# Inverse square roots of the layer norms and of one root mean square: ScalarE's root and VectorE's reciprocal replaced by a power on GpSimd

## The reference, cut to what matters

```python
def _layernorm(x, axis=-1, eps=1e-05):
    m = jnp.mean(x, axis=axis, keepdims=True)
    v = jnp.var(x, axis=axis, keepdims=True)
    return (x - m) / jnp.sqrt(v + eps)

# inside the first attention (16 heads of 8 features, two softmaxes a1 - lam * a2):
out = jnp.einsum('bhst,bhtd->bhsd', a, v)
rms = jnp.sqrt(jnp.mean(out * out, axis=-1, keepdims=True) + EPS)      # EPS = 1e-6
out_n = out / rms * norm_w[None, :, None, :] * (1.0 - LAMBDA_INIT)

x = L0_attn_x
x = _layernorm(x + first_attention(x))
x = _layernorm(x + fp4_feed_forward(x))
x = _layernorm(x + second_attention(x))
x = _layernorm(x + experts(x))       # eight experts, top 1, with a layer norm of its own inside
return x
```

## Time and profile before

| | us |
|---|---|
| runs | 1400.9, 1401.93, 1407.16 |
| median | 1401.93 |
| span of the profiled execution, first to last instruction | 1405.9 |

### The profile page before, as it was taken

One profiled execution on the slowest core, in us unless ns is written; L12 is line 12 of the kernel. 1 busy time (PEld: TensorE's weight loads), 2 busy tenths in 40 slices (PEclk: granted clock), 3 DMA queues, 4 the chain that ended last, 5 costly groups with the idle time before them and its releaser, 6 DMA issues.

```text
span 1405.9 us, 20714 instructions
## 1 busy us (share of the span) xinstructions
PE 1159.2 (82%) x7625; PEld 587.0 (42%) x7625; DVE 798.6 (57%) x1864; ACT 669.1 (48%) x1489; POOL 417.6 (30%) x463
## 2 busy tenths in 40 slices
PE   2588668799898698899988788899988598899686
PEld 1123222334454334444454434445455365455454
DVE  4697449665775665634776575643875521765312
ACT  1178316672663346663574255664375133266132
POOL 2000112204874022002775022000776300577000
PEclk7599656889998679999998769999999699999799
DMA  5700120000030000000030000000000000000000
GB/s 142 180 3 3 63 43 2 1 10 1 19 80 1 1 2 2 2 2 16 1 98 1 1 2 1 2 2 8 0 2 1 0 1 0 9 1 1 1 0 8
DMA packets 30933, 25.07 MB, mean 18 GB/s; under 512 B 12329, under 2 KB 27761, under 8 KB 30065
## 3 DMA queue, kind: packets, MB, share of 16 engines
q1 hardware_dynamic: 30832, 23.75, 6.6%
HBM read 16.01 MB, written 7.34 MB: 17 GB/s over the span
## 4 chain that ended last, share of the span: by engine, by line
PE 62%; DVE 17%; ACT 6%; POOL 5%; SPq 5%; issue 4%; DMA 1%; POOLq 0%; ACTq 0%; DVEq 0%
PE ps L1296 9%; PE ps L1199 9%; PE ps L1194 8%; PE ps L1323 6%; DVE mx L775 6%; PE ps L1279 6%; PE ps L1338 4%; PE ps L1358 4%; PE ps L1368 4%; PE ps L1430 2%; PE ps L1215 2%; SPq L396 2%; POOL PROB L459 2%; PE ps L1254 2%; PE ps L1309 1%
## 5 line engine op out<-in xcount | busy, mean ns | idle before, releaser
L775 DVE TENSOR_REDUCE mx<-ps 128x1 f32<-128x512 f32 x512 | 323.3, 683 | 149.5 <-PE ps L1254 147.6
L1033 ACT ACTIVATE PROB<-ps 128x512 f32<-128x512 f32 x512 | 276.3, 600 | 199.3 <-PE ps L1279 198.2
L459 POOL TENSOR_SCALAR PROB<-PROB,rsum 128x128 f32<-128x128 f32 (+3 forms) x224 | 229.2, 1036 | 58.8 <-DVE rsum L903 58.2
L1075 ACT ACTIVATE PROB<-ps,mx 128x128 f32<-128x128 f32 (+3 forms) x256 | 133.1, 526 | 152.6 <-DVE mx L898 152.4
L1254 PE MATMUL ps<-kst,qst 24*128 24x512 bf16 x512 | 157.5, 461 | 34.9 <-DVE mx L775 20.4
L1296 PE MATMUL ps<-PROB,v 128*32 128x256 f32 x2048 | 173.3, 427 | 2.7 <-ACT OREG L1042 2.3
L440 POOL CAST mparts<-mx 128x16 bf16<-128x16 f32 x32 | 6.3, 197 | 520.9 <-DVE mx L775 520.9
L1279 PE MATMUL ps<-qst,kst 27*128 27x512 bf16 x512 | 129.7, 434 | 28.7 <-DMA qst<-mrow 15.3
L898 DVE TENSOR_REDUCE mx<-ps 128x1 f32<-128x128 f32 (+3 forms) x256 | 112.9, 482 | 70.5 <-PE ps L1341 70.4
L1194 PE MATMUL ps<-xnT,w_sb 128*128 128x512 f32 x256 | 141.8, 659 | 7.2 <-DVE MREG L718 3.7
L995 ACT ACTIVATE MREG<-ps,b_sb 128x512 f32<-128x512 f32 x128 | 88.3, 690 | 121.7 <-PE ps L1194 121.3
(11 more groups left out here) (183 smaller groups left out, 1372.5 us busy)
## 6 DMA issues: line engine op xcount, KB each, us to landing
qk_terms<-RREG SPq DMA_DIRECT2D x48, 128.0 KB, 2.1
kst<-qk_terms SPq DMA_DIRECT2D x16, 192.0 KB
qst<-qk_terms SPq DMA_DIRECT2D x16, 192.0 KB
w_sb<-in_L_ffn_W_dram SPq DMA_DIRECT2D x1, 2048.0 KB
qst<-mrow SPq DMA_DIRECT2D x96, 4.0 KB
ZC<-in_L_attn_x_dram SPq DMA_DIRECT2D x4, 256.0 KB, 3.2
XN<-in_L_attn_x_dram SPq DMA_DIRECT2D x4, 256.0 KB, 9.4
out_dram<-XP SPq DMA_DIRECT2D x4, 256.0 KB, 2.3
```

The source lines that it names most:

```text
L459: pool.tensor_scalar(tile, tile, rsum1[:, 2 * v + half:2 * v + half + 1], None, ALU.mult).then_inc(scaled1, 1)
L775: dve.tensor_reduce(mx0[:, ga % 2, col:col + 1], ps[:, max_banks[MAX_SLOT[n] % len(max_banks)], :], AX, ALU.max, negate=True).then_inc(slo ...
L1033: act.activation(prob0[:, s % 2, q % 4, q % 8 // 4], ps[:, s0_banks[q % len(s0_banks)], :], ACT.Exp, scale=float(HD0) ** -0.5).then_inc(ex ...
L1075: act.activation(prob1[:, half, at:at + w], ps[:, a1_bank(v, half), 0:w], ACT.Exp, bias=mx1[:, col:col + 1], accum_out=sum1[:, col:col + 1 ...
```

## The change

ACT no longer takes any square root. For each of the places above POOL adds the epsilon (for the root mean square it also multiplies by 1/8) and raises the result to the power -0.5, as a power of two tensors, against a tile `root` that is filled with -0.5 at the start. DVE then multiplies by the result and takes no reciprocal. On POOL the new steps stand behind `scale_probs(r, 10)` and the bias add for the root mean square, behind `scale_probs(r, 19)` for the norm after the first attention, and in `overlap` behind `max_parts0(k, 5)` for the norm after the feed-forward, ahead of `max_parts0(k, 0)`, between it and `max_parts0(k, 1)`, and at the end for the three norms of the experts' half.

```diff
-        eps = sb("eps", [P, 2])
+        root = sb("root", [P, 4 * H0])[:, :]
...
@@ block.gpsimd
-            pool.memset(eps[:, 0:1], LN_EPS).then_inc(setup_pool, 1)
-            pool.memset(eps[:, 1:2], RMS_EPS).then_inc(setup_pool, 1)
+            pool.memset(root, -0.5).then_inc(setup_pool, 1)
...
+            def over_std(st, mv, n, var, std):
+
+                pool.wait_ge(var, n)
+                step(pool.tensor_scalar(st, mv[:, :, 1], LN_EPS, None, ALU.add)); settle()
+                pool.tensor_tensor(st, st, root[:, 0:NT], ALU.pow).then_inc(std, 1)
...
             def overlap(r):
-                k = r + 1
+                k, i = r + 1, r - 1
                 hidden = 0 <= r < BATCH
                 if hidden:
                     rounds = quantise(ha, hc, 1408, hq_ready)
+                if 0 <= i:
+                    over_std(stC, mvC, 3 * i + 1, varC, stdC)
                 for g in range(NG):
                     if k < BATCH:
                         max_parts0(k, g)
+                    if 0 <= i and g == 0:
+                        over_std(stC, mvC, 3 * i + 2, varC, stdC)
                     if hidden and g in (2, 3):
...
+                    if hidden and g == 5:
+                        over_std(stB, mvB, 2 * r + 2, varB, stdB)
+                if 0 <= i:
+                    over_std(stC, mvC, 3 * i + 3, varC, stdC)
 
             def turn(k, nx, v, rounds):
...
+                if k < BATCH and v == 10:
+                    pool.wait_ge(ms_ready, k + 1)
+                    step(pool.tensor_scalar(rms[:, 1], rms[:, 0], 1.0 / HD0, RMS_EPS, ALU.mult, ALU.add))
+                    settle()
+                    pool.tensor_tensor(rms[:, 1], rms[:, 1], root, ALU.pow).then_inc(rms_ready, 1)
+                if k < BATCH and v == 19:
+                    over_std(stB, mvB, 2 * k + 1, varB, stdB)
                 if nx < BATCH and v in (10, 13):
                     split_next(nx, (v - 10) // 3)
...
@@ block.vector
             def scale(src, dst, mv, st, std, n, done):
                 dve.wait_ge(std, n)
-                step(dve.reciprocal(st[:, 1], st[:, 0])); settle()
                 for t in range(NT):
-                    ins = dve.tensor_scalar(dst[:, t], src[:, t], mv[:, t, 0:1], st[:, 1, t:t + 1], ALU.subtract, ALU.mult)
+                    ins = dve.tensor_scalar(dst[:, t], src[:, t], mv[:, t, 0:1], st[:, t:t + 1], ALU.subtract, ALU.mult)
...
                 if v == 11:
                     dve.wait_ge(rms_ready, k + 1)
-                    step(dve.reciprocal(rms[:, 0], rms[:, 1]))
...
                 if v == 20:
                     dve.wait_ge(stdB, 2 * k + 1)
-                    step(dve.reciprocal(stB[:, 1], stB[:, 0])); settle()
...
@@ block.scalar
-            def std_b(n):
-                act.wait_ge(varB, n)
-                act.activation(stB[:, 0], mvB[:, :, 1], ACT.Sqrt, bias=eps[:, 0:1]).then_inc(stdB, 1)
-
-            def std_c(n):
-                act.wait_ge(varC, n)
-                act.activation(stC[:, 0], mvC[:, :, 1], ACT.Sqrt, bias=eps[:, 0:1]).then_inc(stdC, 1)
...
-                    if v == 10:
-                        act.wait_ge(ms_ready, k + 1)
-                        act.activation(rms[:, 1], rms[:, 0], ACT.Sqrt, bias=eps[:, 1:2], scale=1.0 / HD0).then_inc(rms_ready, 1)
-                    if v == 19:
-                        std_b(2 * k + 1)
```

More of the change, by code:

```diff
@@ L191, in build @@
         xq = XQ[:, :].rearrange("p (t n) -> p t n", t=NT)
-        bnB, mvB, stB = sb("bnB", [P, NT, 6]), sb("mvB", [P, NT, 2]), sb("stB", [P, 2, NT])
-        bnC, mvC, stC = sb("bnC", [P, NT, 6]), sb("mvC", [P, NT, 2]), sb("stC", [P, 2, NT])
+        bnB, mvB, stB = sb("bnB", [P, NT, 6]), sb("mvB", [P, NT, 2]), sb("stB", [P, NT])[:, :]
+        bnC, mvC, stC = sb("bnC", [P, NT, 6]), sb("mvC", [P, NT, 2]), sb("stC", [P, NT])[:, :]
         PROB = sb("PROB", [P, 2 * 4 * PW])
@@ L417, in _ @@
             pool.memset(kst[:, :, :], 1.0).then_inc(setup_pool, 1)
-            pool.memset(eps[:, 0:1], LN_EPS).then_inc(setup_pool, 1)
-            pool.memset(eps[:, 1:2], RMS_EPS).then_inc(setup_pool, 1)
+            pool.memset(root, -0.5).then_inc(setup_pool, 1)
+            pool.wait_ge(setup_pool, 5)
+            pool.memset(v0[:, :, :, HD0:HD0 + 1], 1.0).then_inc(setup_pool, 1)
             pool.wait_ge(setup_pool, 6)
-            pool.memset(v0[:, :, :, HD0:HD0 + 1], 1.0).then_inc(setup_pool, 1)
-            pool.wait_ge(setup_pool, 7)
             own = [0]
@@ L577, in scales @@
                     last.then_inc(done, 1)
-            dve.wait_ge(setup_pool, 7)
+            dve.wait_ge(setup_pool, 6)
             dve.wait_ge(first_in, 48)
@@ L822, in outputs0 @@
                     dve.wait_ge(rms_ready, k + 1)
-                    step(dve.reciprocal(rms[:, 0], rms[:, 1]))
                 if v == 12:
-                    settle()
-                    w = rms[:, 0].rearrange("p (g a) -> p g a", a=1).broadcast_to([P, 4 * 4 * NT, HD0])
+                    w = rms[:, 1].rearrange("p (g a) -> p g a", a=1).broadcast_to([P, 4 * 4 * NT, HD0])
                     step(dve.tensor_tensor(o0, o0, w, ALU.mult))
@@ L845, in input0 @@
                     dve.wait_ge(stdB, 2 * k + 1)
-                    step(dve.reciprocal(stB[:, 1], stB[:, 0])); settle()
                 if v in (20, 21):
                     for t in (2 * (v - 20), 2 * (v - 20) + 1):
-                        ins = dve.tensor_scalar(XA[:, t], ZB[:, t], mvB[:, t, 0:1], stB[:, 1, t:t + 1], ALU.subtract, ALU.mult)
+                        ins = dve.tensor_scalar(XA[:, t], ZB[:, t], mvB[:, t, 0:1], stB[:, t:t + 1], ALU.subtract, ALU.mult)
                         if t < NT - 1:
@@ L995, in experts_stream @@
                     act.activation(hE[:, f], ps[:, 5 + f % 2, :], ACT.Relu, bias=b1_sb[:, e, f:f + 1]).then_inc(relu_done, 1)
-                if (s, c) == (17, 3):
-                    std_c(3 * i + 3)
             def silu(r, t, bank):
@@ L1011, in ffn_stream @@
                     act.copy(hT[0:96, t % 2, 2, :], ps[0:96, 7, 256:384]).then_inc(hT_ready, 1)
-                if (s, c) == (9, 2):
-                    std_b(2 * r + 2)
                 if (s, c) == (10, 1):
@@ L1048, in turn @@
             def turn(k, nx, v):
-                if k < BATCH:
-                    if v == 10:
-                        act.wait_ge(ms_ready, k + 1)
-                        act.activation(rms[:, 1], rms[:, 0], ACT.Sqrt, bias=eps[:, 1:2], scale=1.0 / HD0).then_inc(rms_ready, 1)
-                    if v == 19:
-                        std_b(2 * k + 1)
                 if nx < BATCH:
```

## The result

The changed kernel takes 1462.82 us (median of four runs, 1460.9 to 1463.66) where the kernel before, run beside it, takes 1404.55 (four runs): a ratio of 1.0404, 95% interval 1.0372 to 1.0436. The profiled execution took 1460.9 us, with a span of 1459.1 us against 1405.9 before. The direction was forecast, the size was not: +15.5 us and a range to 1440.

What follows compares the result with a forecast made beforehand. TensorE carried 62% of the chain, so waits at the 24 root places counted, not ACT or POOL as bounds. Terms 9.9 + 4.5 + 2.4 + 1.75 - 0.8 - 2.2 gave +15.5 us on 1401.9, so 1417 us, range 1390 to 1440.

Steps and rivals of the forecast that it cites:

- x64: Time of POOL's power on 64 columns, for the root mean square: 1.5 us, between 0.32 and 2.8.
- The third rival: The power is done element by element, 10 us at 64 columns: 1456 us or far more; chance 0.12.
- A: Root mean square in the second attention's loop: +3.3 us in each of rounds 0 to 2, nothing in round -1.
- B: Norm after the first attention, v = 19, 20: +1.5 us in each of three rounds; round -1 only a longer hand-over.
- C1: First norm of the experts' half: PE's transpose waits for POOL, +1.2 us in each of rounds 1 and 2.
- hand-overs of B, C1 and C3: Where nothing else is late, DVE's scaling starts 0.85 us after the statistics instead of 0.58: +0.25 us at seven places.
- C3: Last norm of the experts' half: only a longer hand-over, +0.25 us in all four rounds.
- norm after the feed-forward, rounds 1, 2: Gives back most of PE's 1.23 us wait for ACT: 1.0 us gained in each of these rounds.
- the place term of 1.8: At A, DVE's maxima of v = 13 come 1.8 us later, plus x64, from the step's place in POOL's queue.
- The first rival: Loads come off and no wait shows; A gains 2.3 and B 2.4 us a round: 1389 us; chance 0.17.
- The estimate of 1370 us: By the skill page, two loads cost some 5.3 us per root; A and B alone would give 32 us.
- The second rival: PE's other queued work covers most of DVE's lateness; A costs 1, B 0 a round: 1406 us; chance 0.18.

Runs made afterwards that it cites:

- e1: Changed kernel with the 64-column power replaced by a product of the same shape (root mean square left out): 1418.9 us, ratio 1.009 to the kernel before.
- e7: Kernel before, with only the norms after the first attention (ahead of v = 18's products) and after the feed-forward as POOL powers: 1394.58 us, ratio 0.9916.
- e6: e1 with the short root-mean-square step moved ahead of scale_probs(10) and the bias add: 1418.34 us, ratio 1.009 to the kernel before.
- e8: e7 with the root mean square's sum of squares and ACT root moved ahead into the round's projections: 1402.9 us, ratio 0.9975 to the kernel before.
- e5: e1 with the twenty 4-column norm powers also replaced by products, so no root is computed: 1404.48 us, ratio 0.999 to the kernel before.
- e9: e7 with the power for the norm after the first attention moved behind v = 19's products: 1400.5 us, ratio 0.9977 to the kernel before.

## Why the prediction was right in direction and wrong in size

**The step that failed is the price of the power.** It was put "nearer the upper end than the middle of a plain add: x64 = 1.5 us", between bounds of 0.32 and 2.8, and at 0.35 for four columns. It measured 10.57 and 1.04. The upper bound took twelve passes at 3.45 ns a column of an ordinary two-operation form, 41 ns a column; the power takes 159. The row that the bound was scaled from shares nothing with a power but the engine, and a bound made so is none. The third rival, "The power is slow", had x64 at 10 us and 1456 us, with a chance of 0.12; it is what happened, and the sign named for being wrong, a power far from 1.5 us at 64 columns, came. Why a power takes that long no run shows.

With the two measured prices, the prediction's own terms give this, beside the shifts (us; each more than before):

| place | on record | same term, measured price | shift measured |
|---|---|---|---|
| A, rounds 0 to 2 | 3.3 each | 1.8 + 10.57 = 12.4 each | 13.7, 13.5, 14.4 |
| A, round -1 | 0 | 10.57 - 2 = 8.6 | 9.9 |
| B, rounds 0 to 2 | 1.5 each | 1.5 + 0.69 = 2.2 each | 0.3, 1.7, 1.9 |
| C1, rounds 1 and 2 | 1.2 each | 1.9 each | 1.8, 1.8 |
| hand-overs of B, C1 and C3 | 0.25 each | 0.94 each | 0.9 at all seven |
| norm after the feed-forward, rounds 1, 2 | -1.0 each | -0.3 each | -0.35, -0.35 |

The queue reasoning held in its order and its waits, less in its terms. At A in rounds 0 to 2 the shift has grown by 11.4, 11.4 and 11.1 when PE starts again, 1.0 to 1.3 less than the term, as in e1 with a short step (0.9 to 1.1 for 2.1): the place term of 1.8 was too large by about 1. What A shows above that is what the text had named and left out of the sum, the clock, at 0.50 and 0.63 in round 0 after PE's long idle: 2.1 to 3.3 us a round, for the 1 to 3 it gave. At B the term did not come out in round 0: there the clock behind PE's wait is low in both kernels (0.57 over 403 to 411 before, 0.61 over 428 to 436 after), and the shift is 0.3. In round -1 "above x64 of about 2 us the wait comes out" came true. The sum with the measured prices is some 61 us, against 58 in the medians and 53 in the spans; that it is so near is in part that these errors offset each other.

**The count of loads**, 35 off and nine left, and the load at C1 that stays, came out.

**The first rival**, that the loads come off and no wait shows, is false at A and B of this change. Its 2.4 us a round at B exist: e7, with the step ahead in the queue, wins 4.8, 3.2 and 1.9 us in rounds 0 to 2. PE's wait there before was 2.44 us in all three rounds, and the windows of before from its end on are these:

```profile
403.00:411.00 8.00, 7.36 (x31) 4.08 (x33) 3.77 (x10) 3.72 (x12) 3.02 (x4) 0.57 0.30 58
727.00:735.00 8.00, 7.29 (x41) 4.00 (x43) 5.18 (x15) 5.06 (x17) 3.73 (x5) 0.79 0.32 66
1049.00:1057.00 8.00, 7.68 (x59) 4.44 (x59) 5.40 (x18) 5.01 (x17) 5.18 (x6) 1.00 0.01 2
```

Their clock is 0.57, 0.79 and 1.00, and in e7 it is 1.00 in all three rounds. So some 1.9 us of a round is the wait, and the rest the clock. Its 2.3 us a round at A no run shows: there e6 wins 0.4 to 0.7 against before, and e8 1.1 to 2.0 against e7. The estimate of 1370 us from the Trainium skill's page "ScalarE: Activation LUTs" (Table sets: the hidden batching unit) found no support: with all 35 loads off and short steps in place of the powers (e5) the kernel is level with before, the cost of their places included.

**The second rival**, that other work of PE covers the lateness, is false: in the 11 us of POOL's power PE issues nothing.

## What to carry to other kernels

An operation that the trace doesn't show has no upper bound from operations of another kind: before an elementwise function moves to another engine, measure it there at two sizes, since a per-element cost times the columns decides, not the cost of issuing it. Then look at what stands ahead of it in that engine's queue and what stands behind it: the same 1.04 us power won 0.8% when it stood ahead of 4 us of products and 0.2% behind them. A table load taken off is worth what is left when the place of the new step is paid: with 45 us of loads removed (e5) the time was level. With the loads at B off, the step ahead of the products won 4.8 + 3.2 + 1.9 us against before on the shift (e7); behind them, with the same loads off, it won 1.4 in round 0 and lost 0.4 and 2.9 in rounds 1 and 2 (e9).

## What the runs showed of the hardware that was not expected

GpSimd's power of two fp32 tensors on 128 partitions takes 0.40 us and 159 ns a column (1.04 us at 4 columns, 2.93 at 16, 10.57 at 64), where a product of the same shape takes 0.20 at 4 and 0.29 at 64.

TensorE's clock follows a wait for longer than the wait: after 12.60 us of idle at A it was granted 0.50 for 4 us and 0.63 for the next 4; behind a wait of 2.23 us at B (e9) 0.83 over 10 us, and none of this without the wait (e7, 1.00). The wait's length alone does not decide. In the kernel before, PE waits 2.44 us at B in each of rounds 0, 1 and 2, and the 8 us behind have 0.57, 0.79 and 1.00; in e1, behind waits of 2.31, 2.28 and 2.04 us at A, the clock was 1.00 in round 0 and 0.57 for 4 us in rounds 1 and 2. What decides it is open.
